# Half of a sum moved to GpSimd in a DLRM tower: five pairs of slots a tile

## The reference

```python
# B = 2048 samples, 32 fields, D = 64; P = 496 pairs (row < col)
e = stack([tbl_f[ids[:, f]] for f in range(32)], axis=1)        # [B, 32, 64]
p, q = e[:, ROW_IDX], e[:, COL_IDX]                             # [B, 496, 64]
z = einsum('bne,hne,bnh->bn', p, kernel, q)                     # kernel [64, 496, 64]
h = concatenate([z, dense_ctx], axis=1)                         # [B, 512]
h = maximum(h @ W_top1 + b_top1, 0)                             # [B, 512]
h = maximum(h @ W_top2 + b_top2, 0)                             # [B, 256]
y = h @ W_top3                                                  # [B, 1]
```

## Time and profile before

| | |
|---|---|
| median of 3 runs | 962.0 us (961.89 to 962.39) |
| span of the profiled execution, first to last instruction | 790.1 us |
| median less span | 171.9 us |
| PE, VectorE, ScalarE, GpSimd busy | 750.5, 726.6, 712.1, 488.5 us |
| granted clock of TensorE, mean | 0.996 |

### The profile page before, as it was taken

The page is one execution under the profiler, slowest core; times in us unless marked ns, Lnnn a source line. Parts: engine busy times, 40 slices in busy tenths (PEclk is TensorE's granted clock), DMA queues, the critical chain, the costliest instruction groups (busy, mean ns, idle before and its releaser), DMA issues.

```text
span 790.1 us, 23068 instructions
## 1 busy us (share of the span) xinstructions
PE 750.5 (95%) x7700; PEld 514.2 (65%) x7700; DVE 726.6 (92%) x679; ACT 712.1 (90%) x5535; POOL 488.5 (62%) x527
## 2 busy tenths in 40 slices
PE   2877999999999999999999999999999999999998
PEld 1545667666766766766676666767676666766666
DVE  0668999999999999999999999999999999999885
ACT  0568999999999999999999999899999999999985
POOL 7777776666666666666666666666666666665000
PEclk9989999999999999999999999999999999999999
DMA  3871111111111111111111111111111111111000
GB/s 88 257 232 28 29 28 26 26 26 25 25 25 24 25 26 26 24 25 25 24 26 23 26 26 25 24 23 27 25 26 23 25 25 25 25 25 22 2 2 1
DMA packets 29049, 28.39 MB, mean 36 GB/s; under 512 B 15610, under 2 KB 16643, under 8 KB 28931
## 3 DMA queue, kind: packets, MB, share of 16 engines
q0 software_dynamic: 16384, 16.81, 11.2%
q1 hardware_dynamic: 12546, 10.11, 4.4%
HBM read 26.87 MB, written 0.01 MB: 34 GB/s over the span
## 4 chain that ended last, share of the span: by engine, by line
PE 79%; ACT 6%; issue 5%; DVE 4%; POOL 3%; DMA 2%; SPq 1%; DVEq 0%; POOLq 0%
PE T L612 32%; PE T L600 19%; PE psE L559 11%; PE psZ L632 11%; ACT prod L415 5%; PE psE L547 4%; POOL E L350 3%; DVE prod L490 1%; DVE prod_t L469 1%; DVE z L508 1%; PE psZ L627 1%; DMA z<-dense_ctx 1%; DMA E<-tbl,idx 1%; SPq L299 1%; PE psE L554 1%
## 5 line engine op out<-in xcount | busy, mean ns | idle before, releaser
L415 ACT ACTIVATE prod<-prod 128x64 f32<-128x64 f32 x2684 | 642.0, 243 | 12.2 <-DVE prod L487 12.2
L350 POOL DMA_INDIRECT E<-tbl,idx x512 | 483.0, 943 | 238.5 <-issue 98.7
L415 ACT ACTIVATION_READ_ACCUMULATOR prod<-prod 128x1 f32 x2684 | 509.6, 190 | 0.0
L612 PE MATMUL T<-kst,eT 64*128 64x512 f32 (+3 forms) x2304 | 335.8, 420 | 13.9 <-DVE prod L490 5.9
L487 DVE TENSOR_TENSOR prod<-T,E 128x1024 f32<-128x1024 f32 x192 | 230.9, 1216 | 16.3 <-PE T L612 14.3
L600 PEld LDWEIGHTS T<-eT,kst 64*128 64x128 f32 x3072 | 194.9, 189 | 74.9 <-issue 36.2
L469 DVE TENSOR_TENSOR prod_t<-T,eT 128x1024 f32<-128x1024 f32 x192 | 232.0, 1215 | 9.4 <-PE T L600 8.8
L612 PEld LDWEIGHTS T<-kst,eT 64*128 64x128 f32 x2304 | 174.3, 191 | 73.4 <-issue 37.9
L600 PE MATMUL T<-eT,kst 64*128 64x128 f32 x3072 | 213.5, 279 | 2.3 <-issue 1.2
L508 DVE TENSOR_REDUCE z<-prod 128x12 f32<-128x768 f32 (+2 forms) x161 | 168.1, 1045 | 0.0
L490 DVE TENSOR_TENSOR prod<-T,E 128x1024 f32<-128x1024 f32 x64 | 77.9, 1217 | 26.0 <-PE T L612 25.9
(11 more groups left out here) (41 smaller groups left out, 77.4 us busy)
## 6 DMA issues: line engine op xcount, KB each, us to landing
E<-tbl,idx POOLq DMA_INDIRECT x512, 2.4
kst<-K_T SPq DMA_DIRECT2D x28, 256.0 KB, 3.6
w<-W_top SPq DMA_DIRECT2D x1, 1024.0 KB
kst<-K_T SPq DMA_DIRECT2D x4, 192.0 KB, 4.9
w<-W_top SPq DMA_DIRECT2D x1, 512.0 KB
z<-dense_ctx SPq DMA_DIRECT2D x16, 8.0 KB, 2.1
idx<-ids SPq DMA_DIRECT2D x1, 240.0 KB
y_out_dram<-y SPq DMA_DIRECT2D x7, 1.0 KB
```

The source lines that it names most:

```text
L350: nc.gpsimd.indirect_dma_start(out=E[:, u, f, :], out_offset=None, in_=tables[f], in_offset=bass.IndirectOffsetOnAxis(ap=idx[:, t, f:f + 1 ...
L415: last = nc.scalar.activation(x, x, ACT.Copy, accum_out=z[:, t % 2, Z_COLUMNS[s][m]:Z_COLUMNS[s][m] + 1])
L612: last = nc.tensor.matmul(T[:, s_ring(t, s), bank + m * D:bank + (m + w) * D], eT[rows, t % 2, i // 2, :], kst[rows, at + m * D:at + (m + ...
```

## The change

GpSimd adds the two halves (elements 0 to 31 and 32 to 63) of VectorE's share of the products of five pairs of slots a tile, those that end in slots 7, 14, 19, 24 and 27, in place in `prod`. In the last tile the pair (16, 17) is among them. Tiles 0 and 1 are left as they were (`HALVED_FROM = 2`). The addition for slot s stands in GpSimd's queue behind the gather of field s + 1 of the next tile; for the last tile, which has no gathers beside it, the additions stand alone. VectorE then sums 32 elements in place of 64, after a wait for `half_done`, and does so four steps after the pair's second slot (`HALF_LAG`) in place of one; sums stay in order. VectorE's share of slots 12, 14, 21 and 24 rises from 6 to 7 in all tiles, and ScalarE's falls from 10 to 9. Bursts, the z transpose, one group of transposes and MLP steps move by one to three steps (in `LAST_STEP` one entry, l2 of block 1, goes from step 27 to 26).

```diff
-SUM_LAG = 5
+SUM_LAG = 6
+HALVED_SHARE = {12: 7, 14: 7, 21: 7, 24: 7}
+HALVED = (7, 14, 19, 24, 27)
+HALVED_FROM = 2
+HALVED_LAST = (7, 14, 17, 19, 24, 27)
+HALF_LAG = 4
-TR_STEP = (-4, -1, 2, 15)
-Z_STEP = 3
-MLP_STEP = {("l1", 0): (1, 9), ("l1", 1): (1, 18), ("l1", 2): (1, 23), ("l1", 3): (2, 6),
-            ("l2", 0): (2, 10), ("l2", 1): (2, 18), ("l3", 0): (2, 22)}
+TR_STEP = (-2, -1, 2, 15)
+Z_STEP = 4
+MLP_STEP = {('l1', 0): (1, 12), ('l1', 1): (1, 18), ('l1', 2): (1, 24), ('l1', 3): (2, 6), ('l2', 0): (2, 11), ('l2', 1): (2, 18), ('l3', 0): (2, 23)}
+    def halved(t):
+        return () if t < HALVED_FROM else HALVED_LAST if t == TILES - 1 else HALVED
+    def halves_of(t, s):
+        return sum(len(halved(x)) for x in range(t)) + halved(t).index(s) + 1
+    reduce_at, steps = {}, 0
+    for t in range(TILES):
+        for some in REDUCES[t]:
+            steps = max(steps, NS * t + some[-1] + (HALF_LAG if some[-1] in halved(t) else 1))
+            reduce_at.setdefault(steps, []).append((t, some))
...
+            return HALVED_SHARE.get(s, DVE_SHARE[SLOTS[s][0][0]])
...
+            def halve(t, some):
+                k, ring = share(t, some[0]), upright_at[t, some[0]] % SHARED_RING
+                pool.wait_ge(mult_done, NS * t + some[-1] + 1)
+                p = prod[:, ring:ring + len(some), 0:k * D].rearrange("p x (n h) -> p x n h", h=D)
+                nc.gpsimd.tensor_tensor(p[:, :, :, 0:D // 2], p[:, :, :, 0:D // 2], p[:, :, :, D // 2:D], ALU.add).then_inc(half_done, 1)
...
-            for t in range(1, TILES):
+            for t in range(1, TILES + 1):
                 for f in range(NF):
-                    gather(t, f)
+                    if t < TILES:
+                        gather(t, f)
+                    for some in REDUCES[t - 1]:
+                        if some[-1] == f - 1 and some[-1] in halved(t - 1):
+                            halve(t - 1, some)
...
-                dve.wait_ge(mult_done, NS * t + some[-1] + 1)
+                if some[-1] in halved(t):
+                    dve.wait_ge(half_done, halves_of(t, some[-1]))
+                    p = p[:, :, :, 0:D // 2]
+                else:
+                    dve.wait_ge(mult_done, NS * t + some[-1] + 1)
...
-                t, s = (at - 1) // NS, (at - 1) % NS
-                for some in REDUCES[t] if at >= 1 else []:
-                    if some[-1] == s:
-                        reduce(t, some)
+                for t, some in reduce_at.get(at, []):
+                    reduce(t, some)
```

More of the change, by code:

```diff
@@ L46 @@
 MIXED_CROSS = (0, 1, 3)
-TR_STEP = (-4, -1, 2, 15)
-Z_STEP = 3
-MLP_STEP = {("l1", 0): (1, 9), ("l1", 1): (1, 18), ("l1", 2): (1, 23), ("l1", 3): (2, 6),
-            ("l2", 0): (2, 10), ("l2", 1): (2, 18), ("l3", 0): (2, 22)}
-LAST_STEP = {("l1", 0): (1, 10), ("l1", 1): (1, 13), ("l1", 2): (1, 18), ("l1", 3): (1, 20),
-             ("l2", 0): (1, 21), ("l2", 1): (1, 27), ("l3", 0): (1, 28)}
+TR_STEP = (-2, -1, 2, 15)
+Z_STEP = 4
+MLP_STEP = {('l1', 0): (1, 12), ('l1', 1): (1, 18), ('l1', 2): (1, 24), ('l1', 3): (2, 6), ('l2', 0): (2, 11), ('l2', 1): (2, 18), ('l3', 0): (2, 23)}
+LAST_STEP = {('l1', 0): (1, 10), ('l1', 1): (1, 13), ('l1', 2): (1, 18), ('l1', 3): (1, 20), ('l2', 0): (1, 21), ('l2', 1): (1, 26), ('l3', 0): (1, 28)}
 def plan(fields):
@@ L262, in dlrm_tower @@
         mult_done = sem("mult_done")
+        half_done = sem("half_done")
         dve_reduced = sem("dve_reduced")
@@ L272, in share @@
         def share(t, s):
-            return LAST_SHARE.get(s, DVE_SHARE[SLOTS[s][0][0]]) if t == TILES - 1 else DVE_SHARE[SLOTS[s][0][0]]
+            if t == TILES - 1 and s in LAST_SHARE:
+                return LAST_SHARE[s]
+            return HALVED_SHARE.get(s, DVE_SHARE[SLOTS[s][0][0]])
         ends = [T[:, (STEPS - 3 + x) % T_RING, BANK * y:BANK * y + P] for x in range(3) for y in (0, 1)]
```

## The result

Four runs of each kernel: 950.9 us after (945.9 to 953.2), 961.9 before. The ratio of the times is 0.986, 95% interval 0.984 to 0.989, so the change makes the kernel faster by 1.1 to 1.6%. The forecast was 950.5. The number came true; the way to it did not, as the profile after already shows.

A forecast was written before the change was run, and what follows sets the result against it. VectorE (90.6 us a pair) was taken as the bound, PE (89.8) just under. Six pairs -10.5, tile 2 -0.3, tile 1 +0.27, last tile -1.0: sum -11.5, so 962.0 becomes 950.5 us, range 943 to 960.

The forecast's parts named there:

- the runs' median is 171.9 us above that span, and I carry this over: Whole execution: 171.9 us beyond the profiled span of 790.1 us was added unchanged to the predicted span of 778.6.
- The largest need is VectorE's 90.6: Full pair of tiles before the change: VectorE needs 90.6 us, PE 89.8 just under it; the pair lasts 92.54.
- the term of -2.0 us a tile: VectorE's five changed sums a tile: shorter by 2.0 us a tile, its need per pair falling from 90.6 to 86.6.
- I cost these together at nothing: Moved sums, bursts, transposes and MLP steps: no net cost, with half a microsecond a pair to either side.
- My 11.5 us: Whole kernel: the predicted saving, taking the span from 790.1 to 778.6 and the time from 962.0 to 950.5.
- The term of -1.0 us for the last tile: Last tile, six halved sums and no gathers: PE's, with the same hole at the seam, 1.0 us saved.
- the slope of 2.37 ns an element: GpSimd's additions: two reads and a write cost 2.37 ns an element, 5.6 us a tile, net 5.0.
- 44.6: GpSimd's need a tile by the Trainium skill's price of 2.2 ns an element, instead of the forecast's 44.9 us.
- GpSimd did not become the bound: Rival: at 3.2 ns an element GpSimd needs 46.7 us a tile and paces all, 969 us; chance 0.09.
- VectorE never waited for its halves: VectorE waits for GpSimd's halves only if GpSimd is over 2 to 3 us behind; under 0.3 us a pair.
- 44.9 of 45.4: GpSimd's need of 44.9 us a tile with the additions, against z transposes predicted 45.4 us apart.
- that rival: Additions hold up VectorE's products when both engines read SBUF: 49 us a tile, 1000 us in all; chance 0.02.

The follow-up runs named there:

- runs 1 to 4: First group of follow-up experiments, each timed beside the kernel before, whose median there was 962.2 us; later groups had other medians.
- Run 10: Kernel before, with each VectorE sum reading only 8 of the 64 elements: 983.6 us beside 984.3, ratio 1.000.
- run 2: The changed kernel without the halving in any tile; shares of 7 and moved steps stay: 939.2 us, ratio 0.977 to the kernel before.
- run 9: Kernel before with all moved steps, shares of 6 and no halving: 975.5 us beside 984.3, ratio 0.990.
- run 7: Kernel before with SUM_LAG 6 in place of 5, bursts one step later and nothing else: 971.7 us, ratio 1.007.
- run 1: The kernel before, unchanged, profiled again: 962.1 us, ratio 1.000, span 958.1.
- run 8: Kernel before with VectorE's share of slots 12, 14, 21 and 24 at 7 in place of 6, nothing else: 966.4 us, ratio 1.002.

## Why the prediction was right in its number and wrong in its reasons

**The premise failed: "the runs' median is 171.9 us above that span, and I carry this over".** Every execution with a known span since had 1.8 to 2.6 us outside it (952.75 against 950.4, 960.35 against 958.1). The executions of the kernel before that were timed beside runs 1 to 4 had spans near 960 us; the one that was read, 790.1, showed another balance: VectorE almost without idle time, PE's signals on time. The 171.9 us were no fixed offset: all but some 2 of them lie inside the span of a timed execution, and the forecast explains none of them. They were visible before, as the difference of the two numbers in the table. One sentence asking what could take 172 us outside a span would have put every share of busy time in doubt.

**"The largest need is VectorE's 90.6" failed** for the timed executions. Run 10 took 8 us a tile from VectorE and gained nothing; the windows after show VectorE idle a fifth of the time. So the term of -2.0 us a tile, the core of the sum, is worth nothing or less: runs 2 and 9 and the change stand at 0.977, 0.990 and 0.986, and the halving takes 1.0% back where it meets the moved steps. At the old steps it is worth nothing (1.004 with, 1.002 without, intervals overlapping).

**"I cost these together at nothing" failed.** It was said of the moved steps. They carry the gain: 1.0% alone, 2.3% with the shares of 7. My 11.5 us were the wrong terms with the right sum, and the sum was right by luck: in this order of adding them, it was about -1.0% from the steps, -1.4% from the shares on top of them, +1.0% from the halving. The middle term compares run 2 with run 9, which belong to different groups. Nor does each moved step gain: the bursts' alone makes the kernel 0.7% slower (run 7).

**The term of -1.0 us for the last tile failed too, in the one stretch that takes the same time in both executions of the kernel before.** From the last tile's first multiplication to the end the kernel before takes 63.1 us (790.1 less 727.00; run 1 has 958.1 less 895.04) and the change 62.9 (950.4 less 887.47), 0.2 us less.

**What held.** The durations of VectorE's sums and GpSimd's additions; the slope of 2.37 ns an element that I took for the addition is 2.09 by the rows after, (1277 - 1009) / 128, with 0.2 us fixed, and the lengths agree since the two errors cancel. By the price that the prediction takes from the Trainium skill (GPSIMD Engine Reference, "Performance versus the Vector engine") the estimate would be 44.5 us a tile, not 44.6: 2176 x 2.2 ns + 0.45 - 0.65 is 4.6, on top of 39.9. GpSimd did not become the bound (it is busy for 60% of the span), and VectorE never waited for its halves at a distance of four steps; but at 55.7 us a tile GpSimd had some 11 us of room, so this doesn't test the forecast, in which it needed 44.9 of 45.4. Additions beside VectorE's products did not lengthen those (1217 to 1219 ns for 1024 columns in the page after, 1215 to 1217 before), so that rival is out; the Trainium skill (SBUF — State Buffer, "Who interferes with whom") has it so for instructions with at most one input in SBUF, and the trace agrees. The Trainium skill's advice against elementwise adds on GpSimd (GPSIMD Engine Reference, section "When to use GPSIMD") is borne out in the result only, since the change is faster with VectorE summing all 64 elements (run 2).

**What stays open.** In the timed executions PE's results come late and its queue stutters, and the kernel's time reacts to things that change nobody's work, or that change it the other way: five sums moved by three steps are worth 4.4%, GpSimd's additions in front of late short sums gain 3.2%, shorter sums in the same place lose 1.1%. The effects don't add up over the runs, and no theory of mine foretold them: not that VectorE presses PE into more waiting (then run 10 would be slower than before, and it is equal), nor that late sums are bad as such (with GpSimd's additions in front of them, in the change, most of their cost is gone). TensorE's granted clock doesn't order them either: its mean was 0.957 after, 0.970 in run 1, 0.981 in run 8, which is no faster than before, and 0.964 in the fastest kernel; in the page after it falls to 0.93 in stretches such as 400 to 450 us. At the lower of its two levels (1.2 against 2.4 GHz) for twice 4.3% of 950.4 us, the clock after costs PE at most 41 us, not the 160 by which the spans differ. What delays PE's completions, and why one execution was free of it, no run here tells. The nearest lead is in run 1: they are late only while gathers run. A kernel without the gathers, or with them issued earlier, would have tested it and wasn't run; nor is it recorded on which chip or when the execution of 790.1 us was taken. An execution like that one didn't come again, so the change's worth in it, for which the forecast was really made, wasn't measured beyond the last tile.

## What to carry to other kernels

Compare the span of the profiled execution with the times of the runs before reading anything else: here a gap of 18% meant that the trace was of an execution unlike the timed ones, and the balance read from it didn't bound those. Take away an engine's work outright (run 10) before optimizing it; it is one kernel and settles what shares of busy time can't. Look in the slow trace for a stretch that is not slow, and ask what is missing there: here it was the gathers. When a change bundles a new mechanism with a retuned order, time the order without the mechanism: here it was the better kernel, 939.2 us.

## What the runs showed of the hardware that was not expected

- The same program, with VectorE's busy time the same within 1%, ran once in a span of 790.1 us and otherwise in 956 to 971 us (run 1 and beside it). PE's signals came on time in the first; in run 1 VectorE waited up to 19.3 us for one.
- In thirteen traces 308 to 354 of PE's 713 semaphore increments came over 0.2 us late, and none of the 699 that followed the last gather by over 1.3 us. The last tile, without gathers, took 46.12 us in the stretch compared, in the execution of 790.1 us and in run 1.
- In one late stretch PE's queue gave out one or two weight loads, 0.7 us apart (500.36 and 501.08 in run 1's rows), in a burst that has no wait inside it, and then 14 at 502.48.
- A tensor_tensor add of fp32 on GpSimd took 1009, 1145 and 1277 ns for 384, 448 and 512 results, and a gather behind it started after 0.16 us in place of 0.30.
